# Second layer's projection and norm, third layer's norm, table and edge stage in one block, in rounds of four columns of nodes

## The reference

```python
gat_out = agg.reshape(n, H * C) + bias          # second layer: edge sums of 4 heads
proj = gat_out @ Wp + bp
h = x + jax.nn.elu(proj)
mu = jnp.mean(h, axis=-1, keepdims=True)
var = jnp.mean((h - mu) ** 2, axis=-1, keepdims=True)
out = (h - mu) * jax.lax.rsqrt(var + LN_EPS) * gamma + beta
...
x = x + out
h = jnp.maximum(_layernorm(x, axis=-1), 0.0)    # third layer
norm = dis[row] * dis[col]                      # dis = 1 / sqrt(degree)
msg = norm[:, None] * h[row]                    # row: source, col: destination
out = jax.ops.segment_sum(msg, col, num_segments=n) + b   # after a product with W
```

## Time and profile before

| | us |
|---|---|
| median of three runs | 3068.38 |
| the profiled execution | 3063.03 |
| its span, first to last instruction | 3061.3 |
| last addition of the second layer's edge stage ends | 1228.69 |
| block m1 | 1229.00 to 1270.13 |
| block n2 | 1271.67 to 1293.79 |
| first gather of the third layer's edge stage | 1294.71 |
| last gather issued | 1816.55 |

### The profile page before, as it was taken

The page is one execution under the profiler, slowest core; times in us unless marked ns, Lnnn a source line. Parts: engine busy times, 40 slices in busy tenths (PEclk is TensorE's granted clock), DMA queues, the critical chain, the costliest instruction groups (busy, mean ns, idle before and its releaser), DMA issues. The chain is left out here.

```text
span 3061.3 us, 51748 instructions
## 1 busy us (share of the span) xinstructions
PE 2435.5 (80%) x14042; PEld 2054.7 (67%) x14042; DVE 2184.3 (71%) x5057; ACT 903.4 (30%) x2523; POOL 2034.2 (66%) x2115
## 2 busy tenths in 40 slices
PE   5777887525776677487777777999999999999997
PEld 5777877525666666365555555788888888888884
DVE  5555555536888888555555554688888888898885
ACT  1111111136666664111111111233333333233333
POOL 4777777457777772177777755777777777777730
PEclk9777677657878888589999986999999999999996
DMA  3444444133333330045555548988899899999850
GB/s 94 93 88 86 85 86 88 34 68 64 59 60 60 63 56 9 23 144 157 159 159 156 158 144 192 210 200 203 203 212 209 204 201 204 215 200 209 201 120 11
DMA packets 342570, 396.85 MB, mean 130 GB/s; under 512 B 173176, under 2 KB 211814, under 8 KB 342378
## 3 DMA queue, kind: packets, MB, share of 16 engines
q1 hardware_dynamic: 260842, 257.28, 37.3%
q0 software_dynamic: 66560, 82.77, 13.6%
q10 hardware_dynamic: 14976, 54.53, 5.2%
HBM read 333.06 MB, written 61.27 MB: 129 GB/s over the span
## 5 line engine op out<-in xcount | busy, mean ns | idle before, releaser
L1956 PE MATMUL psum<-ckv,z 128*128 128x256 f32 x3328 | 799.3, 388 | 0.0
L1956 PEld LDWEIGHTS psum<-ckv,z 128*128 128x128 f32 x3328 | 609.1, 191 | 110.7 <-issue 35.0
L1788 POOL DMA_INDIRECT ga<-XX,src_i x416 | 400.3, 962 | 171.5 <-issue 126.2
L234 POOL DMA_INDIRECT ga<-TA,src_i x416 | 410.3, 986 | 155.9 <-issue 126.5
L1779 POOL DMA_INDIRECT acc<-QW,dst_i x416 | 402.9, 969 | 160.3 <-issue 115.8
L1033 POOL DMA_INDIRECT ga<-T,src_i x416 | 403.9, 971 | 146.0 <-issue 125.0
L234 POOL DMA_INDIRECT ga<-T,src_i x416 | 395.4, 950 | 149.2 <-issue 124.6
L2072 DVE TENSOR_TENSOR z<-psum,shb 128x2560 f32<-128x2560 f32 x104 | 293.2, 2819 | 51.6 <-PE psum L1943 45.7
L1127 PE MATMUL psum<-HT,wy 128*128 128x128 f32 x1664 | 269.9, 329 | 62.7 <-DVE wy L1400 61.7
L451 PE MATMUL psum<-wre,re 128*128 128x68 f32 x832 | 212.3, 347 | 126.0 <-DVE oneT L296 81.4
L1127 PEld LDWEIGHTS psum<-HT,wy 128*128 128x128 f32 x1664 | 247.4, 236 | 80.8 <-DVE wy L1400 73.8
(11 more groups left out here) (367 smaller groups left out, 4435.0 us busy)
## 6 DMA issues: line engine op xcount, KB each, us to landing
shb<-in_ea SPq DMA_DIRECT2D x104, 640.0 KB
WKV<-wkvo ACTq DMA_DIRECT2D x104, 512.0 KB
shb<-in_ea SPq DMA_DIRECT2D x104, 512.0 KB
wkv<-WKV SPq DMA_DIRECT2D x104, 512.0 KB
dl<-DL SPq DMA_DIRECT2D x208, 128.0 KB
win<-TB SPq DMA_DIRECT2D x416, 32.0 KB
ga<-T,src_i POOLq DMA_INDIRECT x832
ef<-in_ea SPq DMA_DIRECT2D x104, 128.0 KB
```

Of the source, the lines that this page charges most:

```text
L234: pool.indirect_dma_start(o, None, table, bass.IndirectOffsetOnAxis(ap=src_i[:, g * GT + t:g * GT + t + 1], axis=0)).then_inc(s_g[k], 16)
L1788: pool.indirect_dma_start(ga[:, (g % GR) * GT + t, 0:D], None, XX, bass.IndirectOffsetOnAxis(ap=src_i[:, g * GT + t:g * GT + t + 1], axis= ...
L1956: last = pe.matmul(kv_of(k)[:, t, :], z[:, k % 2, j, t * 128:(t + 1) * 128], ckv[:, j, :], start=False, stop=(j == NZ - 2), skip_group_che ...
```

## The change

The blocks m1, n2 and e2 become one block, and `end_of_layer` is called ahead of it, after the second layer's edge stage. Within it:

- The projection goes in seven rounds of four columns (the last has one column), each in its own PSUM bank.
- The norms go in two parts, columns 0 to 15 and 16 to 24 (`MPARTS`). The sums over a node's features are taken round by round for the second layer's norm.
- The squares are ACT's (`squares`, `squares_2`); so is the negative part (`Relu` of `-x`, then `Exp` of its negative). The product with `gamma` is POOL's, on each round.
- The mean is folded into the difference, and the factors `1/std` and `dis` are multiplied first, so that one instruction makes a part of the table in `H`.
- SP loads the weights at the block's start, then the first four tiles `ef`, then stores each part of the table as it is ready. POOL's gathers wait for all four stores (`n2_o`, 64).
- PE transposes each part after its table rows; the seven copies are on ACT behind all its other work; the zeroing of `acc` is on DVE behind the table.

The core of the diff:

```diff
-        layer.close()
-        R1 = rounds(NJ, 8)
...
+        R1 = rounds(NJ, 4)
+        SPLIT = 4
+        MPARTS = [slice(0, 16), slice(16, NJ)]
@@ gpsimd @@
+                pool.memset(w2kv[:], 0.0).then_inc(n2_z, 1)
+                pool.tensor_tensor(X[:], X[:], beta[:].unsqueeze(1).to_broadcast([PN, NJ, D]), ALU.add).then_inc(m1_x, 1)
+                for r, (_, n) in enumerate(R1):
+                    J = round_of(r)
+                    pool.wait_ge(m1_c, r + 1)
+                    pool.tensor_tensor(low[:, J, :], XC[:, J, :], gamma[:].unsqueeze(1).to_broadcast([PN, n, D]),
+                                       ALU.mult).then_inc(m1_g, 1)
+                pool.wait_ge(n2_o, 64)
                 gather_program(ga, pool, T2, D, e2_g, e2_S)
@@ sync @@
...
                 sp.wait_ge(e2_pad, 1)
-                each_group(sp, body)
+                for k in range(ER):
+                    body(0, k)
+                for p, J in enumerate(MPARTS):
+                    sp.wait_ge(n2_y, p + 1)
+                    put_rows(sp, T2.rearrange("(p j) f -> p j f", p=PN)[:, J, :], H[:, J, :], n2_o)
+                for k in range(ER, UG):
+                    body(0, k)
+                with sp.Fori(1, NI) as i:
+                    for k in range(UG):
+                        body(i, k)
@@ tensor @@
+                for r, (j0, n) in enumerate(R1):
+                    for j in range(n):
+                        for a in range(2):
+                            last = pe.matmul(bank[r][0:PN, j * D:(j + 1) * D], node_cols(acc[:, a])[:, j0 + j, :], wst[:, a, :],
+                                             start=a == 0, stop=a == 1)
+                    last.then_inc(m1_t, 1)
+                for r, (j0, n) in enumerate(R1):
+                    pe.wait_ge(n2_y, 1 if r < SPLIT else 2)
+                    for j in range(n):
+                        last = pe.transpose(t_bank(r)[0:D, j * PN:(j + 1) * PN], H[:, j0 + j, :], ident[0:PN, 0:PN])
+                    last.then_inc(n2_t, 1)
+                pe.wait_ge(n2_tc, len(R1))
+                pe.wait_ge(n2_l, 11 * 16)
                 pe.wait_ge(e2_pad, 1)
                 each_group(pe, body)
@@ scalar @@
+                def exponential(r):
+                    J = round_of(r)
+                    act.wait_ge(m1_a, r + 1)
+                    act.activation(low[:, J, :], XC[:, J, :], ACT.Relu, scale=-1.0).then_inc(m1_n, 1)
+                    act.wait_ge(m1_n, r + 1)
+                    act.activation(low[:, J, :], low[:, J, :], ACT.Exp, scale=-1.0).then_inc(m1_e, 1)
+
+                def squares(r):
+                    J = round_of(r)
+                    act.wait_ge(m1_c, r + 1)
+                    act.activation(yn[:, J, :], XC[:, J, :], ACT.Square).then_inc(m1_q, 1)
...
+                act.wait_ge(n2_d, 1)
+                act.activation(st[:, 7, :], st[:, 6, :], ACT.Sqrt).then_inc(n2_deg, 1)
+                exponential(0)
+                exponential(1)
+                squares(0)
+                exponential(2)
+                squares(1)
+                exponential(3)
+                squares(2)
+                squares(3)
+                deviation(0)
+                exponential(4)
+                squares(4)
+                exponential(5)
+                squares(5)
+                squares_2(0)
+                exponential(6)
+                deviation_2(0)
+                squares(6)
+                deviation(1)
+                squares_2(1)
+                deviation_2(1)
+                for r, (j0, n) in enumerate(R1):
+                    act.wait_ge(n2_t, r + 1)
+                    act.activation(node_cols(acc[0:D, 0])[:, j0:j0 + n, :],
...
@@ vector @@
+                def projected(r):
+                    J, n = round_of(r), R1[r][1]
+                    dve.wait_ge(m1_t, r + 1)
+                    dve.tensor_tensor(XC[:, J, :], bank[r][0:PN, 0:n * D].rearrange("p (j f) -> p j f", j=n),
+                                      cb[:].unsqueeze(1).to_broadcast([PN, n, D]), ALU.add).then_inc(m1_a, 1)
+                    dve.wait_ge(m1_a, r + 1)
+                    c.link(dve.scalar_tensor_tensor(H[:, J, :], XC[:, J, :], 0.0, H[:, J, :], ALU.max, ALU.add))
+                def centred(r):
+                    J = round_of(r)
+                    dve.wait_ge(m1_e, r + 1)
+                    c.link(dve.scalar_tensor_tensor(H[:, J, :], low[:, J, :], -1.0, H[:, J, :], ALU.add, ALU.add))
+                    c.link(dve.tensor_reduce(st[:, 0, J], H[:, J, :], AX.X, ALU.add))
+                    dve.scalar_tensor_tensor(XC[:, J, :], bc(st[:, 0, :], J), -1.0 / D, H[:, J, :], ALU.mult, ALU.add).then_inc(m1_c, 1)
+                def square_sums(r):
+                    J = round_of(r)
+                    dve.wait_ge(m1_q, r + 1)
+                    c.link(dve.tensor_reduce(st[:, 2, J], yn[:, J, :], AX.X, ALU.add))
+                def variance(p):
+                    J = MPARTS[p]
+                    dve.tensor_scalar(st[:, 3, J], st[:, 2, J], 1.0 / D, EPS, ALU.mult, ALU.add).then_inc(m1_v, 1)
+                def outputs(p, last):
+                    J = MPARTS[p]
+                    dve.wait_ge(m1_sd, p + 1)
+                    c.link(dve.reciprocal(st[:, 5, J], st[:, 4, J]))
+                    dve.wait_ge(m1_g, last)
+                    c.link(dve.tensor_tensor(low[:, J, :], low[:, J, :], bc(st[:, 5, :], J), ALU.mult))
+                    dve.wait_ge(m1_x, 1)
+                    c.link(dve.tensor_tensor(X[:, J, :], X[:, J, :], low[:, J, :], ALU.add))
+                    c.link(dve.tensor_reduce(s2[:, 0, J], X[:, J, :], AX.X, ALU.add))
+                    dve.scalar_tensor_tensor(XC[:, J, :], bc(s2[:, 0, :], J), -1.0 / D, X[:, J, :], ALU.mult, ALU.add).then_inc(n2_c, 1)
+                def variance_2(p):
+                    J = MPARTS[p]
+                    dve.wait_ge(n2_q, p + 1)
+                    c.link(dve.tensor_reduce(s2[:, 1, J], yn[:, J, :], AX.X, ALU.add))
+                    dve.tensor_scalar(s2[:, 2, J], s2[:, 1, J], 1.0 / D, EPS, ALU.mult, ALU.add).then_inc(n2_v, 1)
+                def table_rows(p):
+                    J = MPARTS[p]
+                    dve.wait_ge(n2_sd, p + 1)
+                    c.link(dve.reciprocal(s2[:, 4, J], s2[:, 3, J]))
+                    c.link(dve.tensor_tensor(s2[:, 5, J], s2[:, 4, J], dis[:, J], ALU.mult))
+                    dve.scalar_tensor_tensor(H[:, J, :], XC[:, J, :], 0.0, bc(s2[:, 5, :], J), ALU.max, ALU.mult).then_inc(n2_y, 1)
+                dve.tensor_scalar(st[:, 6, :], cnt[:], 1.0, None, ALU.add).then_inc(n2_d, 1)
+                dve.memset(w1kv[D:128, :], 0.0).then_inc(n2_z, 1)
                 dve.memset(ef[D:128, :, :], 0.0).then_inc(e2_pad, 1)
+                dve.wait_ge(n2_deg, 1)
+                c.link(dve.reciprocal(dis[:], st[:, 7, :]))
+                projected(0)
+                projected(1)
+                centred(0)
+                projected(2)
+                centred(1)
+                square_sums(0)
+                projected(3)
+                centred(2)
+                square_sums(1)
+                centred(3)
+                square_sums(2)
+                square_sums(3)
+                variance(0)
+                projected(4)
+                outputs(0, SPLIT)
+                centred(4)
+                projected(5)
+                square_sums(4)
+                centred(5)
+                variance_2(0)
+                projected(6)
+                square_sums(5)
+                centred(6)
+                table_rows(0)
+                square_sums(6)
+                variance(1)
+                outputs(1, len(R1))
+                variance_2(1)
+                table_rows(1)
+                dve.wait_ge(m1_t, len(R1))
+                c.link(dve.memset(acc[D:128, 0, :], 0.0))
+                c.link(dve.memset(acc[0:D, 0, N:NW], 0.0))
+                dve.wait_ge(n2_tc, len(R1))
                 each_group(dve, body)
                 add_sums(NI - 1, UG - 1)
                 with_bias(NI - 1, UG - 1)
```

More of the change, by code:

```diff
@@ L1503, in build @@
-        end_of_layer()
+        end_of_layer()
+        R1 = rounds(NJ, 4)
+        SPLIT = 4
+        MPARTS = [slice(0, 16), slice(16, NJ)]
+        (m1_t, m1_dve, m1_a, m1_n, m1_e, m1_c, m1_q, m1_g, m1_v, m1_sd, m1_x) = [sem("m1_" + x) for x in
+            ("t", "dve", "a", "n", "e", "c", "q", "g", "v", "sd", "x")]
         w2t = sb("w2t", [128, D])
@@ L1572, in build @@
-        layer.close()
+        (n2_l, n2_z, n2_c, n2_q, n2_v, n2_sd, n2_d, n2_deg, n2_y, n2_t, n2_tc, n2_o) = [sem("n2_" + x) for x in
+            ("l", "z", "c", "q", "v", "sd", "d", "deg", "y", "t", "tc", "o")]
+        XC = tmp("m1_XC", [PN, NJ, D])
+        yn = tmp("m1_yn", [PN, NJ, D])
+        low = tmp("m1_low", [PN, NJ, D])
+        s2 = tmp("m1_s2", [PN, 6, NJ])
+        t_bank = lambda r: bank[(7 + r) % 8]
+        round_of = lambda r: slice(R1[r][0], sum(R1[r]))
         e2_g = [sem(f"e2_g{k}") for k in range(UG)]
```

(19 more changed lines are left out.)

67 lines of the change are left out of this document (15 added, 52 removed).

## The result

The changed kernel took 3051.82 us in the median of five runs (3047.94 to 3052.95); the kernel before, run beside it, 3068.38 us (3065.53 to 3069.57). The ratio is 0.9948, with a 95% interval of 0.9938 to 0.9959: 16.6 us less (12.6 to 19.0 by the interval), where 15.8 were forecast. The profiled execution took 3051.65 us, its span is 3049.9.

What follows compares the result with a forecast made beforehand. A PE-then-DVE chain delays the first gather, and POOL's gathers pace the edge stage behind it. Border, fourth round, DVE's list, waits and store put that gather at 1278.95, not 1294.71: 3068.38 - 15.8 = 3052.6 us, range 3045 to 3061.

Steps and rivals of the forecast that it cites:

- The place: First gather of the third layer's edge stage: whatever it is moved by, the end moves by; forecast 15.8 us earlier.
- Rival C: Edge stage: something else ends it, so earlier gathers buy nothing; 3068 us, chance 0.05.
- The border: Block border ahead of the projection: end_of_layer costs 1.54 us there in place of 0.31.
- The fourth round: Projection on PE: DVE can read the fourth round 15.2 us after PE's start, at 1245.45.
- Rival B: Projection: PE's clock rises from 0.50, first gather another 6 us earlier; 3046 us, chance 0.04.
- DVE's list: From the fourth round to the last table rows: 26.2 us of work and 4.1 us of waits for ACT.
- POOL's product: Product with gamma on 256 numbers: taken as 0.7 us, between 0.57 and 3.58, so DVE never waits for it.
- The store: From the last table rows to the first gather: 3.2 us, between 2.9 and 4.3.
- The table loads: ACT's five loads: 1.28 us each without a drain; with the skill's 1380 ns drain the gain would be 13 us.
- The work at no cost: SP's loads and ef tiles, transposes and copies: hidden beside PE, the store and the first gathers, costed at nothing.
- Rival D: DVE and ACT in lockstep behind the fourth round: sixteen hops; at 1.4 us each slower by 6 us, 3075; chance 0.04.
- Rival A: Small waits larger (POOL's product, loads, hops, store behind ef tiles): gain 8 to 13 us, 3055 to 3060; chance 0.16.

Runs made afterwards that it cites:

- e9: Changed kernel with 24 memsets of 125x1600 on POOL between the table's store and the first gather: 3084.35 us against 3048.64 for the changed kernel beside it.
- e6: Changed kernel with the table stored in one 781 KB piece when all is ready: first gather 4.59 us behind the table in place of 2.66.
- e3: Changed kernel with the order of ACT's and DVE's lists altered (first part's squares earlier, rounds 4 to 6 read earlier): 3052.36 us against 3053.67 beside it.

## Why the prediction was right

- *The place.* The end follows the first gather one for one: the step on which all rested. e9 shows it, 35.7 us for 35.7, within the spread of its runs. Rival C is out.
- *The border.* 1.54 us from the last addition to the block and 0.03 to PE's start were taken, 1.57 together; it was 1.35.
- *The fourth round.* Taken 15.2 us after PE's start, measured 15.24; the granted clock stayed at 0.50 (1.2 GHz) with PE busy all the time. The Trainium skill (TensorE: Matmul & The Clock Gate, Part 1) would have a busy engine at the upper level; here it was not. Rival B was priced at 6 us; half the products gave 5.3.
- *DVE's list.* From the fourth round's read to the last table rows 30.3 us were forecast and 29.84 measured. The waits were 0.22, 1.43, 0.65, 0.28, 0.75 and 0.28, 3.6 us in place of 4.1, and at the places named. The work was 26.2 us, as forecast; but 0.6 of it are the two instructions held by POOL, which the list did not have, so the rest was counted 0.6 too long. That the two cancel is luck.
- *POOL's product.* Taken 0.7 us out of 0.57 to 3.58, measured 0.73; DVE never waited for it by a semaphore.
- *The store.* Taken 3.2 us between 2.9 and 4.3; it was 2.66, under the lower bound. That bound was a row of another store, with other work around it. The upper bound missed as well: e6 took 4.59. This is the largest miss, 0.5 us.
- *The table loads.* 1.28 us each, with the next activation right behind (1252.31 and 1253.60). The Trainium skill (ScalarE: Activation LUTs, What ACT_TABLE_LOAD costs) adds a drain, and the gain by an estimate from it was 13 us: the trace shows no drain, as before, and the gain was 16.6.
- *The work at no cost.* PE used the first group 6.9 us after the first gather, as before, having waited 2.97 us for that gather; POOL waited 2.1 us for the ring, before 1.8.
- *Rival D* had hops of 1.0 to 1.4 us. The round trip from DVE through a square root on ACT and back left 0.28, the activation of 0.21 included, so a hop is some 0.04. *Rival A* is out with it: POOL's product was short, and the first part's store was issued at 1270.24, 0.02 us behind its table rows, behind no `ef` tile.
- *The number.* The median came 0.8 us from the forecast. The three medians of the changed kernel lie 5 us apart, so that this is so close is luck; the stretch is the fair test.

In the stretch the misses are 0.22 us at the border, 0.46 on DVE's list and 0.54 at the store, less 0.05 at the fourth round: 1.17 us together, 16.93 for the 15.76 of the sum.

## What to carry to other kernels

Where a serial stretch stands in front of a stage with a steady pace, its worth is read at one event, here the first gather, and a delay of known size put there tests that, if it is well above the spread of the runs: 8.9 us left it open, 35.7 did not. Cut such a stretch into pieces that follow a producer's rounds, and list the one engine that remains the bound: each of its instructions, and each wait that it has no other work for. Work taken off that engine is worth only what doesn't come back as a wait for the taker; here some 5 us of DVE's work were traded for a gain of 1.9, and a better order of the lists is worth 2.6 in the stretch.

## What the runs showed that had not been expected

An instruction of DVE with two operands in SBUF took 0.73 us in place of 0.42 when it began while POOL's product was running: it ended 0.28 us after the product's end. A reduction with one operand beside such a product stayed at 0.42 (L1695 at 1252.39, POOL from 1251.92 on). In e3, where DVE's instruction at 1260.15 had begun first, it kept its 0.42 and POOL's product took 0.84:

```profile
1260.15 0.42 DVE L1688 SCALAR_TENSOR_TENSOR H<-m_low,H 125x256 f32<-125x256 f32 x1
...
1260.32 0.84 POOL L1488 TENSOR_TENSOR m_low<-m_XC,gamma 125x256 f32<-125x256 f32 x1 [10.45 <-DVE m_XC L1690]
```

The Trainium skill (SBUF — State Buffer, Who interferes with whom) says so: an instruction of DVE with two SBUF inputs and one of GpSimd that reads SBUF share an interface, and whoever starts second waits until the other is through. The trace agrees as to who waits: 0.3 us more for DVE at both places, 0.1 for POOL in e3. It differs in how long: the second lost less than what was left of the first, 0.31 of 0.45 us and 0.30 of 0.43 on DVE, 0.11 of 0.25 on POOL, each time some 0.14 less.
